# Layer 3 of a four-layer gated cross-attention decoder on one core: its self-attention as one block with three score buffers, its mixture's rows gathered by tile and its results added in DRAM, its cross-attention in the narrow form

## The chip, the cores and the metric

The kernel runs on one core of a Trainium2 chip: TensorE (PE in the profile, its weight loads PEld), VectorE (DVE), ScalarE (ACT), GpSimd (POOL) and SyncE (SP), which here only issues DMAs. The metric is the device time of one execution in microseconds, the median of several runs. All activations are float32, but for the operands of layer 3's self-attention scores, which are split into bfloat16 parts.

## The reference, cut to what matters

2048 tokens (2 sequences of 1024) of 256 features go through four layers; each adds a gated attention and a gated feed-forward part to x. Layers 0 to 2 are not touched. Layer 3:

```python
# attention of layer 3: two blocks, gated as a whole by tanh(g_xattn[3])
x = ln(xx);  x = x + mha(x, x, ..., causal=True);  x = ln(x);  return x + mha(x, ctx, ..., causal=False)
# mha: 16 heads of width 32
a = softmax(q k^T / sqrt(32))          # over all 1024 keys; the causal mask multiplies a AFTER the softmax
o = a v;  x_out = x + o @ li1 + b;  return x_out + gelu(ln3(x_out) @ li2 + b) @ li3 + b

# mixture of layer 3: 8 experts, the best 2 of each token, and a shared expert for all tokens
xn = ln(x); probs = softmax(xn @ router_w); topv, topi = top_k(probs, 2); topv /= topv.sum()
out = sum_e comb[:, e] * swiglu(xn, gate_up_w[e], down_w[e]) + swiglu(xn, shared_gate_up_w, shared_down_w)
swiglu(x, gu, dn): gate, up = split(x @ gu); gate = clip(gate, -10, 10); return silu(gate) * up @ dn
x = x + tanh(g_ffn[3]) * out
```

The cross-attention attends to 64 keys per sequence. An expert's gate_up_w is 256 x 2048, its down_w 1024 x 256; the shared expert's inner width is 256.

## The kernel before

x (tokens on partitions, 16 tiles of 128) stays in SBUF all the time, with two more copies of that size, core["xn"] (normalised) and core["xt"] (features on partitions). In the trace these are x_tokens, xn_tokens and x_features. A stage is a block: each engine runs its own written-out instruction list, and they meet by counting semaphores; a wait holds up everything behind it on its engine. PSUM has 8 banks of 512 float32 columns, ps[:, bank, :]. A stage ends with clear_semaphores, a barrier of all engines. The stages of layer 3 that matter here, in order of time: l3p, l3s, l3a, l3f; between them lie others that are not touched.

**l3p, stage_self_project.** For each of 8 pairs of token tiles (k) it makes q and k in three bfloat16 parts and v, and SP sends them to DRAM in an order by entry (L2070, L2078). An entry is one sequence with 4 heads; there are ENTRIES = 8, and the DRAM tensors have a ninth. For k below 4 the first entries' data are sent twice, the second time to the ninth entry. In the middle of it SP also issues load_entry for entry 0 (L2023, L2025), which brings the operands back for l3s.

**l3s, stage_self_attention.** A unit is one tile of 128 queries of one head; an entry has 32 units. A loop (Fori) of two passes with a barrier runs 4 entries (128 units) in a pass. For a unit v, PE makes scores of 128 x 1024 in two banks (L2292, 4 products), DVE takes the negated maximum (L2390), ACT the exponential with its sum (L2373, an accumulator read behind it), DVE inverts the sum (L2397), POOL multiplies the part right of the diagonal by it (L2273) and cuts the diagonal (L2276), PE turns it by up to 4 transposes into a bank (L2308), ACT (even banks) and DVE (odd banks) store it (L2359, L2361), and PE multiplies by the values (L2326, 32 columns of weights); ACT copies that output (L708) once per 4 units. Scores have 2 pairs of banks (0 to 3), turns banks 4 and 5, outputs banks 6 and 7. Turning lags the scores by TURN = 5 units, the output by OUT = 10, and each unit issues a quarter of it. The order on PE in a unit is scores, turn, quarter of an output; on DVE maximum, store, inverse.

**l3a, stage_attention.** The stage is shared by several layers. It folds q and k weights into the context once for the whole stage (L482, fold_q) and, in the wide form, values and output weights as well (fold_v). Then each tile of 128 tokens takes scores (L499, 8 products of 512 columns), a softmax on DVE and ACT over 16 heads x 64 keys, 8 transposes (L509), and in the wide form one output product of pt with fold_v (L542). In the narrow form, which so far only layer 2 (l2a, width 16) takes, values are kept apart in v_blk, PE makes the heads (L522), ACT copies them (L708, tile heads) and PE multiplies them by the output weights (L533), in chunks of 128 rows: 2 for width 16, 4 for width 32. OUT and TURN are then one larger, and the turn of the next stage's normalised tiles (L222) waits for the heads' copy:

```python
if i >= TURN and (i - TURN) % 2 == 0:
    if narrow:
        pe.wait_ge(heads_stored, min(i - HEADS_OUT + 1, TILES))
    norm_turn(pe, (i - TURN) // 2, tiles_of(core["xn"]))
```

**l3f, stage_experts with top=2.** Logits (L949, L954); softmax, top 2, counts and slots on DVE (L1120 to L1271), with two products on PE for the counts (L959, L961). Each expert's rows are laid out in whole tiles of 256 rows first (15 in all) and half tiles of 128 (9), 24 tiles. When the owners of the tiles are known (L1235) SP starts the experts' weights (L864 and on); when the slots are known POOL scatters each of the 16 token tiles twice into l3f_rows in DRAM (L922, 32 indirect DMAs), which was filled with zeros before. In that time PE, DVE and ACT work on the shared expert (L973, L986, L1276 to L1297). Then a tile is: rows loaded by SP (2 buffers), turned (L999) and scaled by ACT (L1066), 8 steps of the hidden product (L1012; 8 instructions a step, 256 or 128 columns moving, weights of the expert stationary), clip on DVE (L1302), silu on ACT (L1077), product on DVE (L1308), and the output product (L1025) of the tile before, copied by ACT to yt (L708) and sent by POOL to l3f_results (L930). After the last tile POOL gathers each token's two results (L939, 32 indirect DMAs, 4 buffers), DVE adds each with its weight to x (L1322), and SP stores x, tile by tile.

## Time and the profile before

| | before |
|---|---|
| median of 3 runs | 2548.7 us (2547.37 to 2549.26) |
| the profiled execution, its own time | 2524.31 us |
| its span | 2522.6 us |
| mean granted TensorE clock | 0.902 |
| instructions | 36317 |
| l3s: first score to last output copied | 967.0 to 1477.1 us |
| l3a: begin; first scores; the next stage's first product | 1660.8; 1683.6; 1831.6 us |
| l3f: first logits to the end | 1965.6 to 2522.6 us |
| l3f: logits ready; counting products begin | 1975.9; 1982.8 us |
| l3f: PE's last product ends; last gather issued; last addition on DVE | 2469.2; 2513.5; 2516.5 us |
| l3f: first half tile's hidden product | 2365.2 us |

All times below are of the profiled execution, from its span's start. Its own time lies 1.7 us above its span and 24.4 us (1.0%) below the median of the runs. In rows of a timeline the first number is the start, the second the time up to the end of the last of the xN instructions; matmuls overlap, so starts are compared with starts. The number in brackets is the engine's idle time before it, with what ended it.

### The profile page before, as it was taken

Reading aid. Unit: us, or ns where it says so; the run is one execution under the profiler, and the core shown is the slowest. Engines: PE = TensorE matmul, PEld = TensorE weight load, DVE = VectorE, ACT = ScalarE, POOL = GpSimd, SP = SyncE. Lnnn points to the kernel's source line nnn. Section 1 sums busy time; section 2 is a strip of 40 time slices with the busy share of each in tenths; the row PEclk is TensorE's granted clock in tenths of the full one; section 3 lists DMA queues with packets and bytes.
Section 4 is the critical chain, followed back from the end, with each engine's and each line's share of the span. In section 5 each row is a group of like instructions: output and inputs, shape, how many; then the busy total and the mean of one; then the engine's idle time right before and its main releaser. Section 6 shows DMA issues by size and latency. Waiting matters only on the chain. (4 is left out here: it accounts for less than half of the span.)

```text
span 2522.6 us, 36317 instructions
## 1 busy us (share of the span) xinstructions
PE 2047.2 (81%) x11904; PEld 1504.7 (60%) x11904; DVE 1367.6 (54%) x3511; ACT 929.6 (37%) x1859; POOL 710.5 (28%) x1199
## 2 busy tenths in 40 slices
PE   5983974467867677999799979969898589999991
PEld 4661863354444454555455558846687378888991
DVE  4871006535745765888688847757636432222332
ACT  4220321112324346888688843232232112222230
POOL 0223011030130125777577751102330230000005
PEclk9995995578979789999999989979999699999995
DMA  2004531000011286333333430110000525555684
GB/s 87 1 1 150 167 104 28 13 13 14 1 19 12 82 216 165 85 85 85 86 65 92 97 108 11 28 36 1 1 13 1 193 104 175 175 175 175 215 287 115
DMA packets 171504, 219.20 MB, mean 87 GB/s; under 512 B 39911, under 2 KB 133540, under 8 KB 165184
## 3 DMA queue, kind: packets, MB, share of 16 engines
q1 hardware_dynamic: 163344, 196.65, 26.7%
q0 software_dynamic: 7264, 20.31, 2.5%
q8 instruction: 88, 1.44, 0.2%
q14 instruction: 88, 0.72, 0.1%
q10 hardware_dynamic: 720, 0.07, 0.0%
HBM read 171.13 MB, written 46.14 MB: 86 GB/s over the span
## 5 line engine op out<-in xcount | busy, mean ns | idle before, releaser
L2390 DVE TENSOR_REDUCE l3s_mx<-banks 128x1 f32<-128x1024 f32 x256 | 313.1, 1223 | 96.7 <-PE banks L2292 93.8
L2292 PE MATMUL banks<-l_stack 128*128 128x512 bf16 x1024 | 268.1, 385 | 44.1 <-ACT xn_tokens L2373 21.0
L1012 PE MATMUL banks<-l3f_xrt,l3f_w 128*128 128x256 f32 (+1 forms) x1536 | 277.9, 342 | 2.7 <-issue 1.5
L1012 PEld LDWEIGHTS banks<-l3f_xrt,l3f_w 128*128 128x128 f32 x1536 | 249.6, 192 | 29.1 <-issue 3.3
L1302 DVE TENSOR_SCALAR l3f_sg<-banks 128x256 f32<-128x256 f32 (+1 forms) x192 | 72.0, 375 | 287.5 <-PE banks L1012 287.5
L2273 POOL TENSOR_TENSOR xn_tokens<-xn_tokens,l3s_sm 128x1024 f32<-128x1024 f32 (+3 forms) x128 | 201.6, 1575 | 50.3 <-DVE l3s_sm L2397 49.2
L222 PE MATMUL banks<-ident,xn_tokens 128*128 128x128 f32 x320 | 64.7, 338 | 166.8 <-DVE xn_tokens L211 148.0
L2292 PEld LDWEIGHTS banks<-l_stack 128*128 128x128 bf16 x1024 | 80.8, 98 | 163.3 <-ACT xn_tokens L2373 52.6
L2373 ACT ACTIVATE xn_tokens<-banks,l3s_mx 128x1024 f32<-128x1024 f32 x128 | 142.7, 1115 | 46.2 <-DVE l3s_mx L2390 45.1
L222 PEld LDWEIGHTS banks<-ident,xn_tokens 128*128 128x128 f32 x320 | 46.6, 172 | 188.4 <-DVE xn_tokens L211 133.0
L2373 ACT ACTIVATE x_features<-banks,l3s_mx 128x1024 f32<-128x1024 f32 x128 | 143.0, 1117 | 27.9 <-DVE l3s_mx L2390 27.6
L1077 ACT ACTIVATE l3f_sg<-l3f_sg 128x256 f32<-128x256 f32 (+1 forms) x192 | 72.2, 376 | 208.9 <-DVE l3f_sg L1302 208.9
L1025 PE MATMUL banks<-l3f_w,l3f_ht 128*128 128x256 f32 x624 | 138.5, 379 | 0.0
L930 POOL DMA_DIRECT2D l3f_results<-l3f_yt x24 | 15.8, 658 | 410.7 <-ACT l3f_yt L708 410.7
L1025 PEld LDWEIGHTS banks<-l3f_w,l3f_ht 128*128 128x128 f32 x624 | 116.8, 190 | 14.9
L2537 PE MATMUL banks<-x_features,weights 128*128 128x256 f32 x512 | 117.5, 390 | 4.3 <-ACT x_features L235 2.4
L2308 PEld LDWEIGHTS banks<-ident,xn_tokens 128*128 128x128 f32 x832 | 96.5, 140 | 29.1 <-issue 10.2
L2550 PE MATMUL banks<-weights,l3m_ht 128*128 128x256 f32 x512 | 113.2, 379 | 0.4 <-DVE l_x L2605 0.4
L2308 PE MATMUL banks<-ident,xn_tokens 128*128 128x128 f32 x832 | 112.6, 273 | 0.5 <-ACT l3s_pt L2359 0.5
L2537 PEld LDWEIGHTS banks<-x_features,weights 128*128 128x128 f32 x512 | 100.1, 196 | 19.5 <-issue 3.8
L2273 POOL TENSOR_TENSOR x_features<-x_features,l3s_sm 128x128 f32<-128x128 f32 (+3 forms) x128 | 92.4, 722 | 65.6 <-DVE l3s_sm L2397 64.6
L2359 ACT ACTIVATE l3s_pt<-banks 128x384 f32<-128x384 f32 (+2 forms) x192 | 97.0, 505 | 24.2 <-PE banks L2326 18.5
(532 smaller groups left out, 3925.4 us busy)
## 6 DMA issues: line engine op xcount, KB each, us to landing
l3f_w<-in_L_ffn_gate_up_w_dram SPq DMA_DIRECT2D x24, 2048.0 KB, 7.6
l3f_w<-in_L_ffn_down_w_dram SPq DMA_DIRECT2D x24, 1024.0 KB, 6.0
l_stack<-l_q_part SPq DMA_DIRECT2D x72, 256.0 KB, 6.0
l_stack<-l_k_part SPq DMA_DIRECT2D x72, 256.0 KB, 11.4
l0f_w<-in_L_ffn_W_dram SPq DMA_DIRECT2D x16, 1024.0 KB, 5.8
l_q_part<-l_stack SPq DMA_DIRECT2D x24, 256.0 KB, 3.0
l_k_part<-l_stack SPq DMA_DIRECT2D x24, 256.0 KB, 3.7
l3f_rows<-l3f_zero SPq DMA_DIRECT2D x13, 384.0 KB, 4.1
```

Source lines behind the costliest of these rows:

```text
L222: last = nc.tensor.transpose(ps[:, bank, c * PAIR + u * P:c * PAIR + (u + 1) * P], src(2 * j + u)[:, c * P:(c + 1) * P], core["ident"][:, :])
L1012: last = nc.tensor.matmul(ps[:, f % 4, h * PAIR:h * PAIR + size], w1_sb[:, p, dc, h * FF + f * P:h * FF + (f + 1) * P], xrt[:, p, dc, 0:si ...
L1025: last = nc.tensor.matmul(ps[:, 4 + p, u * D:(u + 1) * D], ht[:, p, f, u * P:(u + 1) * P], w2_sb[:, p, f, :], start=(f == 0), stop=(f == F ...
L1077: nc.scalar.activation(sg[:, f % 4, 0:size], sg[:, f % 4, 0:size], ACT.Silu).then_inc(silued, 1)
L2273: nc.gpsimd.tensor_tensor(ex[v % RING][:, si * P:], ex[v % RING][:, si * P:], sm[:, v % RING:v % RING + 1].to_broadcast([P, TOK - si * P]) ...
L2292: last = nc.tensor.matmul(ps[:, 2 * (v % 2) + h, :], stack[p][0][s][:, r, si * P:(si + 1) * P], stack[p][1][s][:, r, h * 512:(h + 1) * 512 ...
L2308: last = nc.tensor.transpose(ps[:, 4 + n % 2, c * P:(c + 1) * P], ex[v % RING][:, (si + c0 + c) * P:(si + c0 + c + 1) * P], core["ident"][ ...
L2359: last = op.activation(dst, src, ACT.Copy)
L2373: nc.scalar.activation(ex[v % RING][:, :], ps[:, 2 * (v % 2):2 * (v % 2) + 2, :].rearrange("p a n -> p (a n)"), ACT.Exp, bias=mx[:, v % RI ...
L2390: nc.vector.tensor_reduce(mx[:, v % RING:v % RING + 1], ps[:, 2 * (v % 2):2 * (v % 2) + 2, :].rearrange("p a n -> p (a n)"), AX_X, ALU.max ...
L2537: last = nc.tensor.matmul(ps[:, n % 4, 0:PAIR], w2[:, dc, f * P:(f + 1) * P], core["xt"][:, dc, PAIR * j:PAIR * (j + 1)], start=(dc == 0), ...
L2550: last = nc.tensor.matmul(ps[:, 4 + k % ring, u * D:(u + 1) * D], ht[:, k % 2, f, u * P:(u + 1) * P], w3[:, f, :], start=(f == 0), stop=(f ...
```

## The change

Three stages are changed.

1. stage_attention: the narrow form is taken from width * 2 <= KEYS on. Width 32 of l3a now takes it. The fold of the values (16 of the 32 folds), their ACT copies and masks go; ctx_twice, 2 value products and v_blk come in.
2. stage_self_attention is one block over 8 entries; scores have three pairs of banks (0 to 5); turns and outputs share banks 6 and 7 in the order in which they are issued (uses); the whole output of 4 units is issued at once, before the turn; its copy is on ACT or DVE by the bank. DVE stores a unit's turn one unit later and ahead of the maximum. POOL's product has one tensor input. In stage_self_project the ninth entry is gone, and with it the second sends for k below 4.
3. stage_top2 replaces stage_experts for layer 3's mixture. xn goes to DRAM at the start. PE begins the shared expert right behind the logits and issues the two counting products behind its sixth hidden product; the shared expert's clip, product and addition are on POOL. In place of the scatter, DVE makes one-hot tables of the slots, PE multiplies them (32 products of 78 columns) into a map from slot to token (place) and weight (share), and POOL gathers each tile's rows from xn. ACT multiplies a tile's results by share; POOL adds them by an indirect DMA into out in DRAM, each such DMA after the one before has landed. x with the shared expert's part is stored to out ahead of the first. Half tiles keep the rows stationary and move 512 columns of weights (8 products), DVE and ACT work on 512 columns at a time, and 8 transposes bring the result back. All loops over tiles are written out.

```diff
-    narrow = width * 4 <= KEYS
+    narrow = width * 2 <= KEYS
```

l3s (the order on PE and on DVE):

```diff
-        with nc.Fori(0, ENTRIES // BODY) as jj:
-                                last = nc.tensor.matmul(ps[:, 2 * (v % 2) + h, :],
+                            last = nc.tensor.matmul(ps[:, 2 * (v % SCORES) + h, :],
...
-                        if TURN <= v < BODY * UNITS + TURN:
-                            turn(v - TURN)
-                        if v >= OUT:
-                            output((v - OUT) // R, (v - OUT) % R)
+                    if v >= OUT and (v - OUT) % R == 0:
+                        output((v - OUT) // R)
+                    if TURN <= v < ENTRIES * UNITS + TURN:
+                        turn(v - TURN)
...
-                        nc.gpsimd.tensor_tensor(ex[v % RING][:, si * P:], ex[v % RING][:, si * P:],
-                                                sm[:, v % RING:v % RING + 1].to_broadcast([P, TOK - si * P]), ALU.mult)
+                    nc.gpsimd.tensor_scalar(ex[v % RING][:, si * P:], ex[v % RING][:, si * P:],
+                                            sm[:, v % RING:v % RING + 1], None, ALU.mult)
...
+                for v in range(ENTRIES * UNITS + OUT + 1):
+                    store_output(dve, nc.vector, v - 1, 1)
+                    if v >= TURN + 1:
+                        store_turned(dve, nc.vector, v - TURN - 1, 1)
+                    if v < ENTRIES * UNITS:
+                        dve.wait_ge(scores_ready, v + 1)
+                        nc.vector.tensor_reduce(mx[:, v % RING:v % RING + 1],
...
```

l3p:

```diff
                     places = [(b * GROUPS, GROUPS)]
-                    if b == 0:
-                        places.append((ENTRIES, 1))
```

l3f (POOL's part for the tiles, PE's order, and the half tiles):

```diff
+                def gather(t):
+                    if t >= 2:
+                        pool.wait_ge(rows_turned, t - 1)
+                    for u in range(units(t)):
+                        at = blocks_through[t] + u
+                        pool.indirect_dma_start(xr[:, t % 2, u, :], None, xn_rows,
+                                                bass.IndirectOffsetOnAxis(ap=place[:, at:at + 1], axis=0),
...
+                def scatter_add(t):
+                    pool.wait_ge(y_stored, t + 1)
+                    for u in range(units(t)):
+                        at = blocks_through[t] + u
+                        if at >= 1:
+                            pool.wait_ge(added, 16 * at)
+                        pool.indirect_dma_start(out_rows, bass.IndirectOffsetOnAxis(ap=place[:, at:at + 1], axis=0),
+                                                yt[:, t % 2, u, :], None, bounds_check=T - 1, oob_is_err=False,
+                                                compute_op=ALU.add).then_inc(added, 16)
...
+                for t in range(tiles):
+                    if t + 2 < tiles:
+                        gather(t + 2)
+                    scatter_add(t)
...
+                for j in range(PAIRS + 2):
+                    if j < PAIRS:
+                        for f in range(SC):
+                            shared_hidden(SC * j + f)
+                    if j == 2:
...
+                        nc.tensor.matmul(ps[:, 5, 0:P], tri[:, :], hots[:, :, :].rearrange("p t e -> p (t e)"),
...
+                    if j >= 2:
+                        shared_output(j - 2)
+
+                pe.wait_ge(spread, 1)
+                for n in range(2 * TILES):
+                    last = nc.tensor.matmul(ps[:, 7, 0:2 * BLOCKS], low_hot[:, n, :],
...
+                    for c in range(2):
+                        pe.wait_ge(hid_stored, banks_free(t, 2 * c + 1))
+                        for h in range(2):
+                            for dc in range(DC):
+                                last = nc.tensor.matmul(ps[:, 2 * c + h, :], xrt[:, p, dc, 0:P],
+                                                        w1_sb[:, p, dc, h * FF + c * 512:h * FF + (c + 1) * 512],
+                                                        start=(dc == 0), stop=(dc == DC - 1))
+                        last.then_inc(hid_ready, 1)
...
+                for t in range(tiles):
+                    hidden(t)
+                    if t + 1 < tiles:
+                        turn(t + 1)
+                    if not whole(t):
+                        turn_half(t, 0)
+                    if t >= 1:
+                        output(t - 1)
+                    if not whole(t):
+                        turn_half(t, 1)
+                output(tiles - 1)
...
+                for t in range(tiles):
+                    clip(t, 0)
+                    for f in range(1, steps_of(t)):
+                        clip(t, f)
+                        multiply(t, f - 1)
+                    multiply(t, steps_of(t) - 1)
```

## Rows read from the trace of the kernel before

**Rows 1.** Busy time by stretch: l2a, l3s, then l3f's full tiles and its half tiles

```profile
640.00:720.00 80.00, 65.32 (x356) 37.59 (x359) 61.53 (x90) 25.50 (x36) 14.10 (x69) 0.90 0.00 1
1000.00:1200.00 200.00, 192.24 (x1824) 109.27 (x1823) 169.97 (x290) 162.70 (x316) 149.65 (x211) 1.00 0.35 80
...
2060.00:2360.00 300.00, 298.52 (x1412) 262.65 (x1411) 89.64 (x235) 69.90 (x160) 9.42 (x13) 1.00 0.49 167
2365.00:2460.00 95.00, 95.00 (x719) 91.26 (x718) 33.80 (x137) 30.62 (x93) 5.28 (x9) 1.00 0.79 280
```

The columns: length, busy PE, PEld, DVE, ACT, POOL (each with its instructions), granted clock, DMA share, GB/s.

**Rows 2.** Groups of l3s by line and shape, 967 to 1478 us

```profile
L2390 DVE TENSOR_REDUCE l3s_mx<-banks 128x1 f32<-128x1024 f32 x256 | 313.1, 1223 | 96.7 <-PE banks L2292 93.8
...
L2373 ACT ACTIVATE x_features<-banks,l3s_mx 128x1024 f32<-128x1024 f32 x128 | 143.0, 1117 | 27.9 <-DVE l3s_mx L2390 27.6
...
L2361 DVE COPY l3s_pt<-banks 128x512 f32<-128x512 f32 x48 | 32.8, 682 | 6.3 <-PE banks L2308 5.7
```

The columns: busy us and mean ns of one; idle before it and what ended that.

**Rows 3.** Busy time of L2390 alone, inside l3s's first pass

```profile
1000.00:1200.00 200.00, 128.45 (x105) 1.00 0.35 80
```

**Rows 4.** Timeline of PE in l3s: first scores of either pass, and the last units

```profile
967.00 2.31 PE L2292 MATMUL banks<-l_stack 128*128 128x512 bf16 x5 [12.04 <-PEq L44]
...
1225.90 3.59 PE L2292 MATMUL banks<-l_stack 128*128 128x512 bf16 x8 [8.15 <-issue]
...
1465.64 1.04 PE L2292 MATMUL banks<-l_stack 128*128 128x512 bf16 x4
...
1467.15 0.42 PE L2326 MATMUL banks<-l3s_pt,l_values_in 128*32 128x128 f32 x8
1467.51 1.04 PE L2292 MATMUL banks<-l_stack 128*128 128x512 bf16 x4
```

**Rows 5.** Timeline of PE: a product of l2a, and a pair of tiles in l3a

```profile
690.03 0.64 PE L522 MATMUL banks<-l2a_pt,l2a_v_blk 128*32 128x128 f32 x16
...
1762.18 3.60 PE L499 MATMUL banks<-l3a_fold_q,x_features 128*128 128x512 f32 x8
...
1766.49 3.62 PE L542 MATMUL banks<-l3a_fold_v,l3a_pt 128*128 128x256 f32 x16
...
1778.14 2.31 PE L499 MATMUL banks<-l3a_fold_q,x_features 128*128 128x512 f32 x5
```

**Rows 6.** Groups of l2a by line, 640 to 720 us (five pairs of tiles)

```profile
L222 PE MATMUL banks<-ident,xn_tokens 128*128 128x128 f32 x20 | 4.5, 367 | 14.2 <-ACT l2a_heads L708 14.2
```

**Rows 7.** Timeline of l3f from the first scatter to the first hidden product

```profile
2003.28 1.14 POOL L922 DMA_INDIRECT l3f_rows<-xn_tokens,l3f_slot  x1 [36.13 <-DVE l3f_slot_f L1271]
...
2043.06 0.98 POOL L922 DMA_INDIRECT l3f_rows<-xn_tokens,l3f_slot  x1 [0.30 <-issue]
...
2050.68 1.62 PE L1012 MATMUL banks<-l3f_xrt,l3f_w 128*128 128x256 f32 x3 [1.20 <-ACT l3f_xrt L1066]
```

**Rows 8.** Timeline of PE: a full tile of l3f, and a half tile

```profile
2090.21 13.98 PE L1012 MATMUL banks<-l3f_xrt,l3f_w 128*128 128x256 f32 x64
...
2104.46 7.07 PE L1025 MATMUL banks<-l3f_w,l3f_ht 128*128 128x256 f32 x32
2111.37 0.81 PE L1012 MATMUL banks<-l3f_xrt,l3f_w 128*128 128x256 f32 x3
...
2390.15 7.31 PE L1012 MATMUL banks<-l3f_xrt,l3f_w 128*128 128x128 f32 x64
...
2397.51 3.62 PE L1025 MATMUL banks<-l3f_w,l3f_ht 128*128 128x256 f32 x16
```

**Rows 9.** Timeline of l3f's end

```profile
2469.31 0.38 ACT L708 ACTIVATE l3f_yt<-banks 128x256 f32<-128x256 f32 x1 [3.07 <-PE banks L1025]
...
2472.90 1.09 POOL L939 DMA_INDIRECT l3f_yg<-l3f_results,l3f_slot  x1 [2.37 <-DMA l3f_results<-l3f_yt]
```

**Rows 10.** Timeline of SP's issues in l3p, at pair k = 4

```profile
922.60 9.22 SPq L2070 DMA_DIRECT2D l_q_part<-l_stack  x3
```

**Rows 11.** DMA issues, 2060 to 2360 us: size, median us to landing

```profile
l3f_results<-l3f_yt POOLq DMA_DIRECT2D x13, 256.0 KB, 6.0
```

More of the change, by code:

```diff
@@ L2089, in sent_before @@
             def sent_before(k):
[L2091 removed]
+                return sum(16 * 8 for q in range(k % 2, k, 2))
             @block.gpsimd
@@ L2399, in stage_self_attention @@
-            clear_semaphores()
-        nc.sync.wait_ge(loaded[0], 16 * LOADS * (ENTRIES // 2 + 1))
-        nc.all_engine_barrier()
+                        n = uses["turn", e, g]
+                        if n >= 2:
+                            pe.wait_ge(stored[n % 2], stored_through(n % 2, n - 2))
+                        for c in range(size):
+                            last = nc.tensor.transpose(ps[:, 6 + n % 2, c * P:(c + 1) * P],
+                                                       ex[v % RING][:, (si + c0 + c) * P:(si + c0 + c + 1) * P],
+                                                       core["ident"][:, :])
```

757 lines of the change are left out of this document (618 added, 139 removed).

## The prediction

> **What bounds the kernel now.** I read the busy time by stretch first, then in each stage the timeline of PE and what ended its waits.
>
> In l3s no engine is full: in 200 us PE is busy for 192, DVE for 170, ACT for 163 [rows 1]. DVE waits 96.7 us over the stage ahead of its maximum L2390, nearly all for the scores L2292 [rows 2], which in turn need a pair of banks that the exponential has left. L2390 starts 105 times in those 200 us [rows 3], so a unit takes 200 / 105 = 1.905 us. That loop holds the rate: scores 4 x 0.216 = 0.87, maximum 1.22, exponential 1.12, its accumulator read and the steps between engines some 0.6, together 3.8 us for two pairs of banks, 1.9 a unit. The last unit of the first pass and the first of the second are far apart: the first pass starts at 967.00, its 128th score should then begin at 967.0 + 127 x 1.905 = 1208.9, and the next pass starts at 1225.90 [rows 4]. The seam costs 17.0 less a unit, 15.1 us.
>
> In l3a a pair of tiles takes 1778.14 - 1762.18 = 15.96 us [rows 5] and PE does not wait. In l2a, the narrow form, PE waits 14.2 us in five pairs for the heads' copy [rows 6], 2.84 a pair, and the granted clock of that stretch is 0.90 [rows 1].
>
> In l3f neither end is PE's. From the first scatter at 2003.28 to the last at 2043.06 POOL issues one indirect DMA per 1.28 us, 32 in all, and the first hidden product comes at 2050.68 [rows 7]. In the tiles PE is full: 298.5 of 300 us, 95 of 95 [rows 1]. A full tile is 2111.37 - 2090.21 = 21.16 us, of which 14.25 are hidden and turn, 6.91 output; a half tile is 7.36 + 16 x 0.216 = 10.82 [rows 8]. After the last output, at 2469.2, there is no more of PE; the gathers begin at 2472.90 [rows 9], and the span ends at 2522.6: a tail of 53.4 us.
>
> **The sends in l3p.** Half of k below 4's sends go. At k = 4 SP starts only at 922.60, and its first three issues take 9.22 us [rows 10]: load_entry and the doubled sends are ahead of it. Eight issues of some 0.5 us less put it 4 us ahead; what is behind it sets the first score of l3s. Bounds 0 (DVE's rate hides it) and -9. I take -4.
>
> **l3s.** The seam of 15.1 goes but for one ramp that both have: -15. The rate: with three pairs the loop of 3.8 us allows 1.27 a unit, so an engine or the shared banks hold next. On DVE the stretch shows 170 / 105 = 1.62 of busy a unit [rows 1], and the outputs that move to it (all outputs fall on the odd bank, since 8 or 6 uses lie between two of them) add 64 x 0.28 / 256 = 0.07 less some even turns: 1.67. PE: 0.87 of scores, 4.5 transposes of 0.13 and 0.28 of output give 1.73 at most, 1.64 where the transposes lie close. POOL has 149.65 / 105 = 1.43 before its cheaper form. Against that, turns and outputs now share two banks. Writing out eight units with these durations, four small outputs an entry make a turn wait until DVE, behind its maximum, has emptied the output's bank: inverse 0.15, copy 0.28, turn 0.5, scores 0.87 then follow in a line. It costs 1.1 to 1.3 us each of them, and I get 14.6 us for the eight, 1.83 a unit. So -255 x (1.905 - 1.83) = -19, and -34 in sum. Bounds: the rate unchanged, -15; DVE's 1.67, -15 - 60 = -75.
>
> **l3a.** Sixteen of 32 folds leave the setup of 22.8 us, 16 x 2 x 0.216 = 6.9; v_blk and two products put back some 2: -5. A tile gives up 3.46 of output (16 instructions of 0.216). It gets the heads, 16 instructions that took 0.64 with 32 columns a tile of the array in l2a [rows 5]; with 64 columns I take 0.9, between that and 16 x 0.13 = 2.1. And 8 of output, 1.72. PE's work of a pair falls to 15.96 - 6.92 + 5.24 = 14.3. Then comes the wait of l2a, 2.84 [rows 6]: the turn L222 stands behind the heads' copy, and behind it on PE stand the next scores. 17.15 a pair, 8 x 1.2 = +9.5, with the setup **+5**. Bounds: all of the wait absorbed by the longer output product, -5 - 8 x 1.66 = -18; heads at 2.1, 16 x 1.2 more, +24.
>
> **l3f, its start.** The counting products now stand behind six hidden products of the shared expert: 6 x 8 x 0.216 = 10.4 us from the logits instead of 6.9, with the copies that pace them some 5 us late. Slots come 5 us later than the 2002 that the first scatter shows [rows 7]. Then on DVE, by 1.2 ns a column of the maximum [rows 2]: splitting 1.0, six tables of 624 columns 4.4, one of 4096 columns 4.9, so 2017.5. PE is busy with the shared expert until about 1975.9 + 192 x 0.216 = 2017.4, with pauses 2021. The map, 64 instructions of 0.13, ends at 2029. place 0.4, two gathers of 1.28 and a landing of 3.0, turn and scale 2.2 by the scatter's pitch and the same two steps [rows 7]: 2038.5 against 2050.68, **-12**. Bounds -8 and -20; the copies and the shared additions on POOL, two tensors a time, are the doubtful part.
>
> **Full tiles.** The work of PE is the same, 21.16. The question is whether rows are there. POOL adds tile t's two halves one after the other and only then gathers tile t + 3: from the end of output(t), ACT 0.76, first addition until it has landed L, second issue 1.0, then 0.3 + 1.28 + 3.0 for the gathers: 6.6 + L. PE needs them 13.8 us (2104.0 - 2090.2) after that end, so L may be 7.2. No row shows an addition in DRAM. Plain stores of 256 KB land in 6.0 with the weights beside them [rows 11], and 2.37 with nothing beside [rows 9]; twice the loaded one, for a read ahead of the write, would be 12. I take 4 to 6, nearest to a plain store of half the size: no stall, 0. At 12 it would be 13 x 4.8 = +62.
>
> The Trainium skill, "DMA: Bandwidth & Descriptors", in its section on the anatomy of one DMA on the gpsimd path, speaks against this part: each DMA carries about 2.0 us that hardly depend on its size, mostly the receipt of the write, longest for DRAM, and here two such receipts are in line in each tile. By its formula 128 KB would take 2.3 us (an estimate), and by that too there is no stall; the loaded 6.0 of this trace is well above it, so the sum would be the same and only the tail 1.2 us shorter.
>
> **Half tiles.** 8 products of 512 columns are as long as 32 of 128: 16 x 0.43 = 6.9 against 7.14. But there are two steps, not eight. After the second, DVE clips it (0.68, a copy of 512 from a bank [rows 2]) and only then multiplies the first (0.68) on which turn_half(0) waits; behind that on PE stands the output of the tile before. PE: 6.9, the next tile's turn 0.22, and turn_half(0) at 8.4; four transposes 0.44, output 3.46, transposes 0.44, so 12.8 instead of 10.82 [rows 8]. 9 x 2.0 = 18, and the last tile has its chain without cover, one more: **+19**. Bounds +9 (DVE keeps up: the transposes alone) and +31 (below).
>
> **Tail.** In place of 53.4 us: store_y 0.4, an addition of 3.5, and the 3.7 that a span has from there (2522.6 less the last addition on DVE, 2516.5, less 2.4 of a store): 7.4. **-46**, bounds -40 and -48.
>
> **Sum.** -4 - 34 + 5 - 12 + 0 + 19 - 46 = -72, a profiled time of 2524.3 - 72 = 2452. The runs' median is 24.4 above the profiled execution's own 2524.3; I keep that distance: 2548.7 - 72 = **2477**.
>
> **Rivals.** (a) l3s runs at DVE's own 1.67 a unit, since its idle 0.28 a unit all went to the scores' wait [rows 2]; the shared banks speak against it. 255 x 0.16 = 41 more: 2436. (b) A small gain: l3s keeps 1.905 (its new bank order costs what the third pair gives), +19, and the idle microsecond of each half tile lowers the granted clock as in l2a, where 18% idle went with 0.90 [rows 1]: 9 x 11.8 x 0.11 = +12. 2508. (c) Slower: additions in DRAM land late under the weights' loads. Each microsecond of L above 7.2 delays 13 tiles by one; at L = 12.7 the gain of 72 is eaten, at 14 it is 2548.7 + 16 = 2565. Against it stands the 6.0 of rows 11. (d) No change: the rows late by just as much, or the tail's landings as long as the gathers were; nothing speaks for it.
>
> **Chances.** Forecast 0.6, its own range 2462 to 2495; (a) 0.15; (b) 0.18; (c) 0.05; (d) 0.02. The range, 2442 to 2510, takes in the far bounds of l3s up to half of (a), and (b). A measurement here tells 0.2%, 5 us, from no change. Faster 0.93, same 0.02, slower 0.05.
>
> **What would show it.** L2390's count in 200 us of l3s: 109 at 1.83, 105 if nothing, 120 in (a); no gap at its middle. In l3a a wait of L222 on the heads. The first hidden product at some 12 us less after the logits. Full tiles of 21.16 with L999's wait on the rows absent; if it is there, (c). PE waiting about a microsecond for DVE in each half tile, and the granted clock. Less than 9 us between PE's last product and the end. The prediction is wrong if an indirect addition takes over 7 us to land, or if POOL's shared-expert work, not DVE's tables, holds the map.

## The result, and the profile after

The changed kernel takes 2565.27 us (median of 4 runs, 2563.32 to 2568.79) against 2548.03 for the kernel before: 1.0078 of its time, 95% interval 1.0063 to 1.0094. It is 0.8% slower; forecast were 2477 us and a chance of 0.93 for faster. The profiled execution's own time is 2563.32 us, its span 2561.6. In stages, from either trace (the anchors of before are those of the tables and rows ahead of the prediction):

| stretch | before | after | difference | forecast |
|---|---|---|---|---|
| start to l3s's first scores | 967.0 | 962.8 | -4.2 | -4 |
| l3s: to the next stage's first product | 531.2 | 575.3 | +44.1 | -34 |
| to l3f's first logits (l3a in it) | 467.4 | 463.7 | -3.7 | +5 |
| to the first hidden product | 85.1 | 86.3 | +1.3 | -12 |
| full tiles, to the first half tile | 314.5 | 319.0 | +4.5 | 0 |
| half tiles, to PE's end | 104.0 | 142.9 | +38.9 | +19 |
| tail | 53.4 | 11.5 | -41.9 | -46 |
| sum | 2522.6 | 2561.6 | +39.0 | -72 |

The sum of the traces, +39, is not the +17 of the runs. On some occasions every run of the kernel before takes 2541 to 2553 us and on others 2520 to 2526; its profile is from one of the latter, the timed runs of both kernels are from one of the former. Experiment 2 shows where the 24 us lie.

**l3s.** First the page's lines of the maximum and of POOL's product after, then the busy time by stretch, whole and of the maximum L3018 alone:

```profile
L3018 DVE TENSOR_REDUCE l3s_mx<-banks 128x1 f32<-128x1024 f32 x256 | 311.3, 1218 | 75.9 <-PE banks L2917 75.1
L2902 POOL TENSOR_SCALAR xn_tokens<-xn_tokens,l3s_sm 128x1024 f32<-128x1024 f32 (+3 forms) x128 | 302.9, 2367 | 15.4 <-DVE l3s_sm L3023 15.4
```

```profile
1000.00:1200.00 200.00, 167.65 (x1650) 102.03 (x1643) 153.36 (x269) 144.23 (x269) 187.35 (x187) 1.00 0.33 76
```

```profile
1000.00:1200.00 200.00, 113.29 (x94) 1.00 0.33 76
```

The maximum starts 94 times in 200 us, before 105 times [rows 3]: 2.13 us a unit. DVE, ACT and PE are all less busy than before [rows 1]; POOL, 149.65 before, is busy for 187 of 200 us and has waited for nothing since its first unit (the 15.4 us are one wait). It is the bound.

**l3a.** PE's timeline, the turn and the first scores of a pair, and the next pair's:

```profile
1801.54 0.66 PE L222 MATMUL banks<-ident,xn_tokens 128*128 128x128 f32 x4 [1.28 <-ACT l3a_heads L708]
1802.03 3.60 PE L499 MATMUL banks<-l3a_fold_q,x_features 128*128 128x512 f32 x8
...
1806.43 1.09 PE L522 MATMUL banks<-l3a_pt,l3a_v_blk 128*64 128x128 f32 x16
...
1817.99 0.66 PE L222 MATMUL banks<-ident,xn_tokens 128*128 128x128 f32 x4 [1.28 <-ACT l3a_heads L708]
1818.48 3.60 PE L499 MATMUL banks<-l3a_fold_q,x_features 128*128 128x512 f32 x8
```

A pair takes 16.45 us (15.96 in [rows 5]); the wait for the heads' copy is there, but 1.28 us, not 2.84 [rows 6]. The whole stretch of 463.7 us is 458.6 to 462.1 in the eleven traces below that keep this l3a, so 2 to 5 us of it are the spread between executions.

**l3f's start.** DVE and POOL in the timeline, and PE with the map; then the stretches before and in the map:

```profile
2023.20 0.29 DVE L1801 COPY l3f_total<-banks 128x128 f32<-128x128 f32 x1 [2.73 <-PE banks L1581]
...
2025.70 1.27 POOL L1494 TENSOR_TENSOR x_tokens<-x_tokens,l3f_so 128x512 f32<-128x512 f32 x1 [2.77 <-ACT l3f_so L1695]
2025.79 1.20 DVE L1834 COPY l3f_rows_f<-l3f_scan 128x8 f32<-128x8 f32 x1
...
2066.32 13.94 PE L1588 MATMUL banks<-l3f_spot,xn_tokens 128*128 128x78 f32 x64 [9.44 <-DVE xn_tokens L1916]
...
2088.14 4.17 PE L1619 MATMUL banks<-l3f_xrt,l3f_w 128*128 128x256 f32 x10 [1.21 <-ACT l3f_xrt L1713]
```

```profile
2057.00:2066.00 9.00, 0.00 (x0) 0.00 (x0) 8.85 (x7) 0.61 (x1) 1.26 (x1) 0.72 1.04 395
2066.00:2080.00 14.00, 13.68 (x64) 13.68 (x64) 0.27 (x1) 0.00 (x0) 0.00 (x0) 0.50 0.57 194
```

Two things show. DVE's copy of 8 columns takes 1.20 us and ends where POOL's addition does. The same goes for others in this stretch: 0.41 us beside POOL's clip of 0.40, 0.74 beside its product of 0.73, and 0.17 where POOL does nothing. And PE, which had no work for 9.4 us, does the map at a granted clock of 0.50, 1.2 GHz: 13.9 us for 64 instructions, where I had 8.

**The tiles.** First PE in the full tiles (start and turn of one, start of the next, and the turn at which PE's wait is long enough to be listed):

```profile
2319.97 13.98 PE L1619 MATMUL banks<-l3f_xrt,l3f_w 128*128 128x256 f32 x64
2334.05 0.66 PE L1599 MATMUL banks<-ident,l3f_xr 128*128 128x128 f32 x4
...
2341.45 13.98 PE L1619 MATMUL banks<-l3f_xrt,l3f_w 128*128 128x256 f32 x64
...
2378.83 0.65 PE L1599 MATMUL banks<-ident,l3f_xr 128*128 128x128 f32 x4 [1.90 <-DMA l3f_xr<-l3f_xn,l3f_place]
```

A full tile takes 21.48 us where it took 21.16 [rows 8]: the turn starts 14.08 us behind the tile's first product, and 13.8 behind it when the gathers are further ahead (experiment 3). Now POOL's timeline around the first half tile, then PE's, then an undisturbed half tile with DVE:

```profile
2408.99 1.58 POOL L1520 DMA_INDIRECT out_dram<-l3f_yt,l3f_place  x1 [11.98 <-ACT l3f_yt L1737]
2415.09 1.56 POOL L1520 DMA_INDIRECT out_dram<-l3f_yt,l3f_place  x1 [4.52 <-DMA out_dram<-l3f_yt,l3f_place]
2416.96 1.07 POOL L1510 DMA_INDIRECT l3f_xr<-l3f_xn,l3f_place  x1 [0.30 <-issue]
```

```profile
2407.17 7.03 PE L1628 MATMUL banks<-l3f_w,l3f_xrt 128*128 128x512 f32 x16
2423.37 0.69 PE L1599 MATMUL banks<-ident,l3f_xr 128*128 128x128 f32 x2 [9.16 <-DMA l3f_xr<-l3f_xn,l3f_place]
...
2449.21 0.69 PE L1599 MATMUL banks<-ident,l3f_xr 128*128 128x128 f32 x2 [9.37 <-DMA l3f_xr<-l3f_xn,l3f_place]
...
2464.33 0.66 PE L1639 MATMUL banks<-ident,l3f_hh 128*128 128x128 f32 x4 [1.16 <-DVE l3f_hh L1940]
```

An addition in DRAM lands 6.1 us after its start (2408.99 to 2415.09, with 1.6 of issue in it). Of the 15 that POOL waited for, 14 took 5.9 to 6.2 us and one 7.9 (2364.81 to 2372.73); behind that one PE has the 1.90 us of waiting shown above. So in the full tiles the rows come just too late. At the first half tile they come much too late: PE starts the hidden product at 2407.17 and has done it 6.9 us later, but the gather of the next tile stands behind the two additions of the full tile before and starts at 2416.96; PE has its rows 6.4 us later. PE waits 9.16 us, and one tile on 9.37. An undisturbed half tile takes 12.80 us (hidden products begin at 2455.92 and 2468.72), with the 1.16 us of waiting for DVE in it: this is the forecast 12.8.

### The profile page after: what moved, and what is told of

It is laid out like the page before. It is cut to its first block and busy times, and to the rows that moved or that the text cites. A ratio compares the mean times of both kernels' runs of the same rounds, so it can differ in the third digit from the quotient of the medians.

```text
span 2561.6 us, 34951 instructions
## 1 busy us (share of the span) xinstructions
PE 2045.4 (80%) x11700; PEld 1481.5 (58%) x11700; DVE 1350.3 (53%) x3368; ACT 944.9 (37%) x1829; POOL 909.5 (36%) x1235
## 5 line engine op out<-in xcount | busy, mean ns | idle before, releaser
L3018 DVE TENSOR_REDUCE l3s_mx<-banks 128x1 f32<-128x1024 f32 x256 | 311.3, 1218 | 75.9 <-PE banks L2917 75.1
L2902 POOL TENSOR_SCALAR xn_tokens<-xn_tokens,l3s_sm 128x1024 f32<-128x1024 f32 (+3 forms) x128 | 302.9, 2367 | 15.4 <-DVE l3s_sm L3023 15.4
L1619 PE MATMUL banks<-l3f_xrt,l3f_w 128*128 128x256 f32 x960 | 211.6, 381 | 2.7 <-issue 1.5
L222 PE MATMUL banks<-ident,xn_tokens 128*128 128x128 f32 x320 | 65.0, 339 | 172.3 <-DVE xn_tokens L211 146.7
L1619 PEld LDWEIGHTS banks<-l3f_xrt,l3f_w 128*128 128x128 f32 x960 | 183.5, 191 | 28.5 <-issue 3.3
L1520 POOL DMA_INDIRECT out_dram<-l3f_yt,l3f_place x39 | 62.1, 1593 | 355.7 <-ACT l3f_yt L1737 287.1
L2933 PE MATMUL banks<-ident,xn_tokens 128*128 128x128 f32 x832 | 126.1, 282 | 68.7 <-POOL xn_tokens L2905 60.6
L1926 DVE TENSOR_SCALAR l3f_sg<-banks 128x256 f32<-128x256 f32 x120 | 50.9, 425 | 227.1 <-PE banks L1619 227.1
L2933 PEld LDWEIGHTS banks<-ident,xn_tokens 128*128 128x128 f32 x832 | 89.3, 140 | 124.9 <-POOL xn_tokens L2905 100.4
L3007 ACT ACTIVATE xn_tokens<-banks,l3s_mx 128x1024 f32<-128x1024 f32 x128 | 142.3, 1112 | 33.3 <-DVE l3s_mx L3018 33.2
L2977 ACT ACTIVATE l3s_pt<-banks 128x384 f32<-128x384 f32 (+3 forms) x224 | 109.5, 489 | 115.3 <-PE banks L2933 114.6
L2917 PEld LDWEIGHTS banks<-l_stack 128*128 128x128 bf16 x1024 | 101.2, 99 | 82.0 <-issue 16.5
L2902 POOL TENSOR_SCALAR x_features<-x_features,l3s_sm 128x128 f32<-128x128 f32 (+3 forms) x128 | 139.0, 1086 | 0.1
L2979 DVE COPY l3s_pt<-banks 128x384 f32<-128x384 f32 (+3 forms) x160 | 88.1, 551 | 55.8 <-PE banks L2933 54.7
```

The source lines that it names most:

```text
L222: last = nc.tensor.transpose(ps[:, bank, c * PAIR + u * P:c * PAIR + (u + 1) * P], src(2 * j + u)[:, c * P:(c + 1) * P], core["ident"][:, :])
L1619: last = nc.tensor.matmul(ps[:, f % 4, h * PAIR:(h + 1) * PAIR], w1_sb[:, p, dc, h * FF + f * P:h * FF + (f + 1) * P], xrt[:, p, dc, :], s ...
L2902: nc.gpsimd.tensor_scalar(ex[v % RING][:, si * P:], ex[v % RING][:, si * P:], sm[:, v % RING:v % RING + 1], None, ALU.mult)
L2917: last = nc.tensor.matmul(ps[:, 2 * (v % SCORES) + h, :], stack[p][0][s][:, r, si * P:(si + 1) * P], stack[p][1][s][:, r, h * 512:(h + 1) ...
L2933: last = nc.tensor.transpose(ps[:, 6 + n % 2, c * P:(c + 1) * P], ex[v % RING][:, (si + c0 + c) * P:(si + c0 + c + 1) * P], core["ident"][ ...
L2977: last = op.activation(dst, src, ACT.Copy)
```

## The experiments

**1. POOL's product with two tensor inputs.**

```diff
-                    nc.gpsimd.tensor_scalar(ex[v % RING][:, si * P:], ex[v % RING][:, si * P:],
-                                            sm[:, v % RING:v % RING + 1], None, ALU.mult)
+                    nc.gpsimd.tensor_tensor(ex[v % RING][:, si * P:], ex[v % RING][:, si * P:],
+                                            sm[:, v % RING:v % RING + 1].to_broadcast([P, TOK - si * P]), ALU.mult)
```

> The changed kernel, with POOL's product in l3s taken back to the form with two tensor inputs (tensor_tensor with the sum broadcast). Theory A, the one-input form with a scalar read from SBUF is slower in itself: it took 2847 ns for 1024 columns against 1895 before, and POOL was busy 187 of 200 us. Then POOL's product falls to 1895 ns, the maximum is started some 109 times in 200 us instead of 94, and the stage from its first scores to the next stage's first product falls from 575 us to about 500: median about 2490. Rival B, POOL's operation is slow because DVE and ACT now run denser beside it: the product stays above 2.5 us for 1024 columns, and the stage stays within 10 us of 575.

Measured: 2497.03 us, 0.9795 of before (0.9772 to 0.9819), 68 us less than the changed kernel. POOL's group of 1024 columns, and the maximum by stretch:

```profile
L2902 POOL TENSOR_TENSOR xn_tokens<-xn_tokens,l3s_sm 128x1024 f32<-128x1024 f32 x32 | 60.6, 1895 | 15.8 <-DVE l3s_sm L3023 15.4
```

```profile
1000.00:1200.00 200.00, 128.77 (x107) 1.00 0.35 80
```

Theory A holds: the operation has its 1895 ns again, with DVE busy for 170.0 and ACT for 162.8 of 200 us, as before [rows 1]. l3s takes 512.2 us (965.8 to 1478.0), 63 less. It gains 19 on the kernel before, not the 34 forecast: 1.88 us a unit instead of 1.83. The other 5 of the 68 us are the spread between executions: in the traces they lie in stretches that this edit does not touch.

**2. The same edit alone, in the kernel before**: L2273 in the one-input form, nothing else.

> The kernel before, with only POOL's product in l3s in the one-input form. Theory A: 2847 ns for 1024 columns here too; POOL needs 1.73 + 0.29 + 0.2 us a unit on average, more than the 1.905 us of the stage, so the stage (531 us from its first scores to the next stage's first product) becomes some 30 to 60 us longer. Rival B: the product keeps its 1895 ns and the stage its 531 us.

Measured: one run, 2611.46 us, 65 above the 2546.54 of the kernel before beside it. 1024 columns take 2846 ns. l3s takes 594.5 us (968.7 to 1563.2) instead of 531.2: +63. One operation's form, alone, is the loss. This trace also shows what the profile of before did not have. DVE in l3f, in the shared expert:

```profile
2096.16 0.42 DVE L1276 TENSOR_SCALAR l3f_sg<-banks 128x256 f32<-128x256 f32 x1 [10.51 <-remote]
...
2110.19 0.43 DVE L1276 TENSOR_SCALAR l3f_sg<-banks 128x256 f32<-128x256 f32 x1 [13.60 <-remote]
```

DVE stands still for 24 us in all, with PE's results there; from the logits' transposes to the first hidden product it is 100.4 us (2037.98 to 2138.38), in the trace of before 75.9. The other stretches outside l3s agree within 2 us. POOL issues its scatters all through the first of the two waits and until 2.8 us before the second ends; whether they are the cause was not tried.

**3. Gathers two tiles further ahead.** POOL's order in l3f:

```diff
                 pool.wait_ge(begun, 16 * PAIRS)
+                gather(2)
+                gather(3)
                 for t in range(tiles):
-                    if t + 2 < tiles:
-                        gather(t + 2)
+                    if t + 4 < tiles:
+                        gather(t + 4)
                     scatter_add(t)
```

> The changed kernel, with POOL issuing the gather of tile t + 4 ahead of the addition of tile t (before: the gather of tile t + 2). Theory: the two waits of PE on rows at the first half tiles, 9.16 and 9.37 us, are there because those gathers stand behind two additions in line; they go, and with them the clock's fall behind them, so that from the first half tile's hidden product to PE's end it takes about 121 us instead of 142.6; the full tiles lose up to 4 us; in all 20 to 25 us less. Rival: the gathers land late because of the weights' loads, whatever their place: the waits stay above 5 us each.

Measured: one run, 2536.66 us, 28.6 less. PE at the first half tile:

```profile
2400.06 7.03 PE L1630 MATMUL banks<-l3f_w,l3f_xrt 128*128 128x512 f32 x16
2406.93 0.38 PE L1601 MATMUL banks<-ident,l3f_xr 128*128 128x128 f32 x2
2408.47 0.66 PE L1641 MATMUL banks<-ident,l3f_hh 128*128 128x128 f32 x4 [1.16 <-DVE l3f_hh L1942]
```

Behind the first tile no wait on rows is left; the half tiles take 123 us instead of 142.9, the full ones 313.6 instead of 319.0, with 21.16 us a tile again. The place of the gather in POOL's queue is what makes PE wait. Its slow landing there (6.4 and 7.0 us for the two gathers that PE waits for at the half tiles, 2.8 behind a full tile's second gather) makes the two waits longer, but makes none by itself.

**4. DVE's order in a half tile.**

```diff
                     for f in range(1, steps_of(t)):
-                        clip(t, f)
-                        multiply(t, f - 1)
+                        if whole(t):
+                            clip(t, f)
+                            multiply(t, f - 1)
+                        else:
+                            multiply(t, f - 1)
+                            clip(t, f)
```

> The changed kernel, with DVE's order in a half tile clip 0, multiply 0, clip 1, multiply 1 instead of clip 0, clip 1, multiply 0, multiply 1. Theory: PE's 1.16 us of waiting for DVE in each half tile is the multiply behind the second clip; an undisturbed half tile falls from 12.80 to about 11.5 us. Rival: the second half then comes later and the wait only moves to the second turn: 12.8 stays.

Measured: one run, 2560.77 us, 4.5 less. PE:

```profile
2455.39 7.03 PE L1628 MATMUL banks<-l3f_w,l3f_xrt 128*128 128x512 f32 x16
2462.26 0.38 PE L1599 MATMUL banks<-ident,l3f_xr 128*128 128x128 f32 x2
2462.48 0.60 PE L1639 MATMUL banks<-ident,l3f_hh 128*128 128x128 f32 x4
...
2466.81 7.03 PE L1628 MATMUL banks<-l3f_w,l3f_xrt 128*128 128x512 f32 x16
2476.24 0.44 PE L1599 MATMUL banks<-ident,l3f_xr 128*128 128x128 f32 x2 [2.40 <-DMA l3f_xr<-l3f_xn,l3f_place]
```

The wait for DVE is gone and this half tile takes 11.42 us; but the next one waits 2.40 us for rows. In all the half tiles take 141.4 us instead of 142.9: alone the edit gives back most of what it wins, and 3 of the 4.5 us are not its own.

**5. and 6. All together, with half tiles in either form.** Both have the edits of 1 and 3. The first gives half tiles the form of before (8 steps, weights stationary, 128 columns moving), the second keeps 512 columns with the order of 4.

> The changed kernel with three edits: POOL's two-input product in l3s, the gathers two tiles further ahead, and half tiles in the form of before (weights stationary, 8 steps of 128 columns). From the two first edits alone 2497 - 28 = 2469. Theory: a half tile takes 10.82 us as before instead of 12.80, its gathers are in time now, so 9 x 2.0 = 18 us less: about 2450. Rival: at 10.8 us a half tile the additions and gathers of POOL (some 1.6 + 1.1 us of issue, then 6 us to land) are late again and PE waits at every second tile: 2460 or more.

> As the run beside it, but with the half tiles of the changed kernel (512 columns moving) and DVE's order clip 0, multiply 0, clip 1, multiply 1. Theory: 11.42 us a half tile without the waits on rows that it had without the earlier gathers: 9 x 0.6 = 5 us above the run beside it, about 2456. Rival: the two forms are equal within 2 us.

Measured: 2450.31 us, 0.9622 (0.9597 to 0.9646), and 2457.04, 0.9651 (0.9625 to 0.9677). In the first a half tile takes 10.82 us (2381.67 to 2392.49) with no wait on rows. Both theories hold. The medians are 6.7 us apart, but the intervals overlap; the traces tell the forms apart: 104.2 us for the half tiles in the old form, 110.6 in the new.

**7. POOL's part of the shared expert on 8 columns.** The clip, the product and the addition work on 8 columns only, so the rest of the shared expert's activations and of its addition is left out; s_ht is set to zero once.

> The changed kernel, with POOL's three operations of the shared expert (clip, product, addition) on 8 columns instead of 256 or 512; it leaves out the rest of the shared expert's activations and of its addition to x. Theory: DVE's small operations that turn counts into tiles stand still while POOL works (a copy of 8 columns took 1.20 us beside a POOL addition of 1.27 us), so without POOL's load DVE's way from the counts to the one-hot tables gets some 10 to 14 us shorter, and so does the time from the logits to the first hidden product (77.6 us). Rival: DVE's waits come from PE, which issues the counting products late and the map behind the shared expert: under 3 us.

Measured: one run, 2541.11 us, 24 less. DVE's same copy, and the stretch of the map:

```profile
2018.42 0.17 DVE L1836 COPY l3f_rows_f<-l3f_scan 128x8 f32<-128x8 f32 x1
```

```profile
2049.00:2056.00 7.00, 7.00 (x65) 7.00 (x63) 0.00 (x0) 0.69 (x1) 0.20 (x1) 1.00 0.81 284
```

From the counts' copy to the one-hot tables it takes 28.1 us (2015.84 to 2043.9) instead of 43.1 (2023.20 to 2066.3). PE's gap ahead of the map goes too, so its clock stays at 1.00 (2.4 GHz) and the map takes 7.0 us. From the shared expert's first product to the first hidden product it is 59.4 us instead of 76.1, 16.7 less and a little more than expected; most of the rest of the 24 lies ahead of l3f, where the edit does nothing. Of DVE's 15 us PE can use 10: the map starts 33.5 us behind the second counting product instead of 43.5, and the shared expert keeps PE busy up to it. What is measured is POOL's width and the gap together; the map's 7 us come with the gap. The Trainium skill, "SBUF — State Buffer", section "SBUF: two separate sides", says that VectorE and GpSimd share one pair of ports as an exclusive lock, held for a whole instruction, and names DVE operations with two SBUF inputs and those in a two-port mode. The rows agree that it waits for the whole operation: 1.20 us beside a POOL operation of 1.27, 0.17 without. The copy has one SBUF input, and no trace shows in which mode it ran.

**8. The product by a constant.** `sm[:, ...]` becomes 1.0 in the one-input form, which leaves out the division by the softmax's sum.

> The changed kernel, with POOL's product in l3s in the one-input form by a constant 1.0 instead of by the sum read from SBUF; it leaves out the division by the softmax's sum. Theory C, the slow part is the scalar read from SBUF: 1024 columns fall from 2847 ns to about 1500 (the clip by constants in l3f takes 0.40 us for 256). Theory D, the one-input form is slow for itself on this engine at float32: 2847 ns stays.

Measured: one run, 2536.45 us. 1024 columns take 2770 ns instead of 2847: theory D. The scalar from SBUF costs 80 ns (128 columns: 528 ns, 608 with it), not the slope. l3s takes 554.2 us, 21 less than 575.3, and 256 operations of 0.08 us are 20.5: what POOL's operation costs goes into the stage one for one.

**9. Four forms of POOL's operation in one kernel**, by head; the second leaves out the division:

```diff
+                    if v % R == 0:
+                        nc.gpsimd.tensor_tensor(src, src, by.to_broadcast([P, TOK - si * P]), ALU.mult)
+                    elif v % R == 1:
+                        nc.gpsimd.tensor_scalar(src, src, 10.0, -10.0, ALU.min, ALU.max)
+                    elif v % R == 2:
+                        nc.gpsimd.tensor_scalar(src, src, 10.0, by, ALU.min, ALU.mult)
+                    else:
+                        nc.gpsimd.tensor_scalar(src, src, by, None, ALU.mult)
```

> The changed kernel, with POOL's operation in l3s in four forms, one for each of the four heads of an entry: two tensor inputs; minimum and maximum with constants (as the shared expert's clip); minimum with a constant, then product with the sum; product with the sum. The second form leaves out the division by the sum for a quarter of the heads. For 1024 columns, theory D1 (the one-input form is slow whatever it computes): about 1.9, 2.8, 2.9, 2.85 us. Theory D2 (only the product in the one-input form is slow, a minimum is not): about 1.9, 1.5, 2.9, 2.85.

Measured: the groups of 1024 columns, in the order of their cost:

```profile
L2908 POOL TENSOR_SCALAR xn_tokens<-xn_tokens,l3s_sm 128x1024 f32<-128x1024 f32 x8 | 29.7, 3714 | 0.8
L2910 POOL TENSOR_SCALAR xn_tokens<-xn_tokens,l3s_sm 128x1024 f32<-128x1024 f32 x8 | 22.8, 2848 | 0.0
...
L2904 POOL TENSOR_TENSOR xn_tokens<-xn_tokens,l3s_sm 128x1024 f32<-128x1024 f32 x8 | 15.2, 1895 | 15.4 <-DVE l3s_sm L3030 15.4
...
L2906 POOL TENSOR_SCALAR xn_tokens<-xn_tokens 128x1024 f32<-128x1024 f32 x8 | 8.3, 1042 | 0.7
```

Theory D2: the one-input form is the fastest of all with minimum and maximum (1042 ns), and slow with a product (2848), on the same tiles in the same stage. Two of its numbers missed: 1.04 us where 1.5 was expected, and 3.71 for the minimum with a product where 2.9 was. With 128 columns they take 294 and 608 ns, the two-input product 401: by the difference over 896 columns 0.83, 2.50 and 1.67 ns a column.

**10. The kernel before once more.**

> The kernel before once more, for its trace. The one that the prediction was made from had 2524.3 us, its timed runs 2548. Theory: the 24 us lie in l3f between the counts and the first hidden product, where DVE stood still for 10.5 and 13.6 us in the trace of the run with only POOL's form changed; from the last logits' transposes to the first hidden product it is then about 99 us in this trace, not 75. Rival: they are spread over the span.

Measured: 2523.35 us, beside another run of the kernel before at 2522.36. The expectation missed: the trace has 75.8 us where I expected 99, as the first one. This run and experiments 1 to 4, beside which the kernel before took 2546.54, were on the chip of the same number, 5, so the difference is not shown to go with the chip. Experiment 2's trace is the only one of the old l3f from an occasion of the longer time, and the only one that shows the 24 us.

**11. l3a wide again**, in the version of 5 (`narrow = width * 4 <= KEYS`).

> The version at 2450 us, with l3a back in its wide form. The traces give the narrow form 3.7 us less in all (setup 5.4 less, a pair of tiles 16.45 instead of 15.96), so 3 to 5 us more here: 2454. Rival: within 1 us, because what follows takes the time back.

Measured: 2457.41 us, 0.9657 (0.9641 to 0.9673), against 0.9622 (0.9597 to 0.9646): some 7 us more, on the theory's side and above its 3 to 5. The intervals touch, so the traces have to tell: from the product behind l3s to l3f's first logits it is 469.7 us with the wide form and 460.7 in the version of 5, 9 us more. The narrow form gains.

**12. The counting products earlier**, in the version of 5: `if j == 1` for `if j == 2`.

> The version at 2450 us, with the two counting products of l3f behind the fourth hidden product of the shared expert instead of the sixth. Theory: DVE waits 2.7 us for them, so the way to the one-hot tables gets 2.7 to 3.5 us shorter: 2447. Rival: PE then waits for DVE's choice instead and the shared expert ends later: no change.

Measured: 2445.71 us, 0.9613 (0.9596 to 0.9629). By the medians 4.6 us less, but the intervals overlap, so the runs alone don't settle it. The traces do: from the logits' transposes to the first hidden product 72.8 us (1941.8 to 2014.6) instead of 77.1 (1944.2 to 2021.3), 4.3 us for the 2.7 to 3.5 expected. PE's wait ahead of the map is 2.48 us here instead of 9.44, and the map still takes 13.1 us, at a granted clock of 0.54, most of it 1.2 GHz; in the 7.6 us before it PE was busy for 3.6.

**13. and 14. l3s: the output one unit later, and two pairs of score banks**, both in the version of 12. `OUT = TURN + R + 2`; `SCORES = 2`.

> The version at 2446 us, with OUT one unit larger in l3s (TURN + R + 2). Theory: of the 15 us that l3s gains less than forecast, most is PE's wait for DVE's last store of a turn ahead of the output (22.1 us idle before the output product, in 64 outputs); one unit later it is there, and l3s gets 10 to 20 us shorter: about 2432. Rival: the output one unit later takes the shared banks from the turns instead, and the wait moves to the transposes: within 3 us.

> The version at 2446 us, with two pairs of banks for the scores in l3s instead of three; turns and outputs still share two banks and the stage is still one block. Theory: the loop scores, maximum, exponential holds two pairs at 1.9 us a unit, and the shared banks add to it: 1.95 to 2.05 a unit instead of 1.88, 18 to 45 us more. Rival: the shared banks, not the loop, hold the rate either way: within 5 us.

Measured, beside runs of the kernel before at 2522.94: 2439.11 us, 0.9673 (0.9657 to 0.9689), and 2495.36, 0.9896 (0.9877 to 0.9914). From first to last scores l3s takes 469.9 and 527.7 us, in the version of 12 479.6: 1.84, 2.07 and 1.88 us a unit. PE's groups in 12, then with the output later, then with two pairs:

```profile
L2939 PE MATMUL banks<-ident,xn_tokens 128*128 128x128 f32 x832 | 128.8, 280 | 11.6 <-ACT l3s_pt L2983 7.7 <-DVE weights L3000 3.7 <-DVE l3s_pt L2985 0.2
L2951 PE MATMUL banks<-l3s_pt,l_values_in 128*32 128x128 f32 x2304 | 77.9, 277 | 22.1 <-DVE l3s_pt L2985 21.3 <-ACT l3s_pt L2983 0.7
```

```profile
L2939 PE MATMUL banks<-ident,xn_tokens 128*128 128x128 f32 x832 | 121.3, 278 | 31.7 <-DVE l3s_pt L2985 21.1 <-DVE weights L3000 10.1 <-ACT l3s_pt L2983 0.4
L2951 PE MATMUL banks<-l3s_pt,l_values_in 128*32 128x128 f32 x2304 | 76.2, 275 | 1.5 <-ACT l3s_pt L2983 0.9
```

```profile
L2923 PE MATMUL banks<-l_stack 128*128 128x512 bf16 x1024 | 269.0, 386 | 64.1 <-ACT xn_tokens L3013 42.9 <-PEq L44 12.4 <-ACT x_features L3013 7.7
```

The output's wait for DVE's last store falls from 22.1 to 1.5 us, but the transposes' wait grows from 11.6 to 31.7: both the theory and its rival are in part right, and l3s gains 9.7 us up to its last scores, 12.3 up to the next stage's first product, the low end of the 10 to 20 expected. With two pairs the scores wait for the exponential again (before, the maximum waited for them [rows 2]), and the stage is 48 us longer, just above the 18 to 45 expected: the third pair carries the gain, and with two pairs the new order would be slower than the old one's 1.905.

## Why the prediction was wrong

**l3s, the step that failed (-34, measured +44).** The prediction wrote "POOL has 149.65 / 105 = 1.43 before its cheaper form". No row of the trace showed that form; I took it as cheaper, gave it no bounds, and listed no rival in which POOL becomes the bound. It costs 2847 ns where 1895 were, which makes POOL's unit 2.0 us and more. Experiments 1 and 2 take the edit out and put it in alone: -68 and +65 us, of which l3s has 63 either way. In both orders of the stage the slow form gives 2.13 us a unit. Without it the total would have been 2497, faster and inside the range, but not because the sum was right: the trace of experiment 1 is 27 us below that of before, not 72, and the other 24 are those of the base (below). In place of -34 there were then -19. The seam's 15 came as forecast; the rate is 1.88 instead of 1.83 a unit, -6 for -19; and 2.5 us are lost from the last scores to the next stage's product (33.2 for 30.7). The rate was missed since the output product, issued ahead of the turn, meets a store that DVE makes one unit later, which my eight units did not hold: experiment 13 takes nearly all of that wait away, 22.1 to 1.5 us, and l3s gets 9.7 us shorter.

**The rows of the half tiles (0; experiment 3 gives back 19.7 us in the half tiles and 5.4 in the full ones).** My sum for the gathers, 6.6 + L, was too short. L is 6.1, just above the forecast's 4 to 6, and within the 7.2 that the sum allowed; but the rest is 8.0, not 6.6. From the output product's end to the first addition's start it is 1.86 us where I had 0.76; and the second addition takes 1.6 of issue, not 1.0; the gathers, 4.5 us with their landing, are as forecast there. That makes 14.1 us against 13.8, so each full tile has 0.3 us more, and with the 1.9 of the one slow landing these are the 5.4 us. The larger miss is at the half tiles. The sum was made with the full tile's 13.8 us. At the first two half tiles the additions are still those of a full tile and PE needs the rows after 6.9. I looked at each kind of tile, not at the seam between them. Rival (c) had the mechanism, and put it at the wrong place: its 2565 us, for a landing of 14 us, are the measured 2565.27 by coincidence. The half tile itself, 12.80, is the forecast's to 0.1 us, and so is its cause, the wait for DVE: 9 x 2.0. With 18.5 us of waits and what the clock lost behind them (the 16 output instructions at 2450.55 take 5.1 us instead of 3.6) the stretch has +38.9.

**l3f's start (-12, measured +1.3).** The counting products came 10.5 us behind the shared expert's first product (2012.09 to 2022.56), as worked out. From the counts to the tables I had 18 + 10.3 = 28.3, which is what it takes without POOL's load (28.1, experiment 7); it took 43.1, because DVE's small operations stood behind POOL's, and the map took 13.9 instead of 8 at half the clock. Experiment 7 gives both back. The prediction named POOL's load as the doubtful part and gave it a bound of -8, too near.

**l3a (+5, measured -3.7, and -5 to -9 by the other traces)**: a mis-sized term. The setup gained 5.4 as forecast; the wait for the heads was 1.28 us, not the 2.84 of l2a. I read this as the longer output product covering a part of it, the bound that I had named; no run tests it. PE's own work of a pair was 0.9 us above my 14.3, in the heads (1.02 us a tile for 0.9), the output (1.83 for 1.72) and the steps around the wait.

**Right**: l3p (-4.2 for -4), the tail (-41.9 for -46), no change of PE's work in the full tiles. In the tail 10.2 us pass from the last addition's start to the end, where I had 3.5 + 3.7; how they split between the landing and the rest no row shows.

**Slips in the sums**, none of which changes the outcome: the terms beside L are 0.76 + 1.0 + 0.3 + 1.28 + 3.0 = 6.3, not 6.6; the steps behind the map add up to 2037, not 2038.5, so l3f's start should have been -13; and the tail is 0.4 + 3.5 + 3.7 = 7.6, not 7.4.

**The base.** The trace gave 75.9 us for a stretch that takes some 100 on other occasions. Against those the change gains some 24 us more than the table shows, which is why the runs say +17 and the traces +39. The new l3f does not have the difference: the version of 12, run where the kernel before took 2545.74, and the version of 13, run where it took 2522.94, both have 81.6 us from l3f's first logits to its first hidden product. What DVE waits for in the old one is named "remote" and is not settled, nor is what tells the occasions apart.

## What to carry to other kernels

An engine with room to spare is only as safe as its next operation: before one form is exchanged for another on an engine that is 75% busy, find that form in some trace or bound it from above, and ask which price makes the engine the bound (here 1.88 us a unit, and GpSimd's 1.43 was 0.45 away from it). Where loops are cut into kinds of pieces, check each producer's due time at the seam, where the last long piece's leftovers meet the first short piece's deadline. The version of experiment 13 with the two-input product, earlier gathers, the old half tile and earlier counts, with the output one unit later, takes 0.9673 of the time of before, 2439.11 us against 2522.94.

## What the hardware showed that I had not expected

- GpSimd in float32: a one-input product takes 2.50 ns a column, by a constant or by a scalar from SBUF, a two-input product 1.67, a one-input minimum and maximum 0.83 (experiments 8 and 9).
- DVE's operations on 8 columns take as long as the GpSimd operation beside them: 1.20 us beside 1.27, 0.74 beside 0.73, 0.41 beside 0.40, and 0.17 alone (experiment 7). The maximum in l3s, which reads PSUM, did not suffer: 1218 and 1216 ns beside GpSimd's slow and its faster form.
- An indirect DMA that adds float32 rows in DRAM is 1.6 us of GpSimd's issue, where a gather is 1.0 to 1.1, and 128 rows of 1 KB land 5.9 to 6.2 us after its start beside the weights' loads, once 7.9. PE had the rows of two gathers in that traffic 6.4 and 7.0 us after their start, and those of the full tiles' gathers after 2.8.
- After 9.4 us without work PE ran 64 instructions at a granted clock of 0.50, in 13.9 us instead of 7.0. After a wait of 2.48 us, behind a stretch in which it had been busy for 3.6 of 7.6, they took 13.1 us at 0.54 (experiment 12).
